# Summing the routed results of a two-layer mixture-of-experts kernel: TensorE takes six token tiles in pairs, VectorE ten, and ScalarE scales every anchor's result

## The chip, the cores and the metric

The kernel runs on one core of a Trainium2 chip. The metric is the device time of one execution in microseconds. In three runs the kernel before took 939.09, 937.78 and 936.85 us, a median of 937.78 us.

## The reference, cut to what matters

The network has two layers on 2048 tokens of width 256. Each layer is a cross attention followed by a mixture of experts, each added to its input. The change lies in the second layer's mixture of experts:

```python
x = x + L0_xattn(layernorm(x), ctx) ; x = x + L0_moe(layernorm(x))
x = x + L1_xattn(layernorm(x), ctx) ; x = x + L1_moe(layernorm(x))
...
# L1_moe, for 32 routed experts (6 per token) and 16 anchors (1 per token)
eo = (silu(x @ w_gate[e]) * (x @ w_up[e])) @ w_down[e]
routed = sum over the token's 6 experts of weight * eo
anchor = (silu(x @ a_gate[l]) * (x @ a_up[l])) @ a_down[l], l from the token's first expert
out = routed + shared + 0.1 * anchor
```

All of it is in float32.

## The kernel before, in words

The last stage handles the tokens of the second layer in gathered tiles of 128 rows: `T1` = 127 routed tiles, then `TA` = 31 anchor tiles, `NTL` = 158 in all (`ORDER` keeps their order). All engines run a loop over i, and each does the step of another tile in it.

- **SyncE** loads the gathered rows of tile i into the ring `RX` of eight buffers (L1054), 16 of the anchor tiles ahead into `RA`.
- **TensorE**, iteration i: it transposes tile i's rows (L859 to L863, two transposes at L332 and L333), multiplies gate and up of tile i-2 (`mm`, L328) and down of tile i-4 (L882). The transposed rows go to one of the three PSUM banks 0, 1 and 6 (`turned1`), so that transposing tile i waits for VectorE's copy of tile i-3. Gate and up are in banks 2, 3 and 7, down in banks 4 and 5.
- **VectorE**, iteration i: it scales the result of tile i-5 if that is an odd tile (`scale_odd`, L2107), copies tile i's transposed rows out (L2121), finds weights and destinations once per four tiles (`find`, L2083 to L2099), and multiplies silu(gate) by up for tile i-3 (L2131, anchors L2133).
- **ScalarE**, iteration i: it scales the result of tile i-5 if that is an even tile (`scale_even`, L1460), copies tile i+1's expert weights to a fixed place (`weights_copy`, L1451), and takes silu of tile i-2 (L1476, anchors L1478).
- **GpSimd** scatters each scaled result with an indirect DMA (L1134) to the tensor `yb1`, where each token has six places, or for an anchor to `yba`, where it has one. A scaled result stands in one of `NYT` = 6 buffers (`YTS`). `result(i)` gives the buffer and how many times its semaphore has counted; before a buffer is written again, the scatter that read it must have landed. `all_back` waits for the landing of the last six scatters, one per buffer.

When the results of all routed tiles are in `yb1`, SyncE loads them back (`yf_load(n)`, L1069) into `YF`, two token tiles of 128 at a time with 1536 values per row, in the order n = 2, 3, 6, 0, 1, 7, 4, 5. The last five of these loads stand in the queue among the last row loads of the ring, and so wait for them: n = 0, 1, 7 each come behind two of them, 4 and 5 behind 7. When the anchors' results have all landed too, it loads those (`YA`, L1090), four token tiles per load, groups 1, 0, 3, 2.

The sixteen token tiles of the output are then summed on two engines. VectorE takes the eleven of `DONE`: for each one add of 768 columns and three of 256 (`yf_add`, L2056 to L2068). It is a generator, of which one step (of five per tile) is taken in each iteration from i = 139, and what is left runs after the loop. Three adds of `YA` (L2144) then finish groups 1, 0 and 2. TensorE takes the five of `SUMMED` after its loop: for each it multiplies the identity by `X` (L890), by the six parts of `YF` (L894) and by `YA` (L897), into one PSUM bank, and ScalarE copies the bank to `X` (L1481). ScalarE sends groups 3 and 2 of the output (L1484), SyncE groups 1 and 0 (L1093).

Of the kernel before, what the change touches and what calls it, by code (L numbers as in the profile page):

```python
# [13 lines left out]
D = 256  # L14
# [5 lines left out]
E0 = 64  # L20
# [9 lines left out]
NEW = 22  # L30
EARLY, BESIDE = 1, 3
FRONT, HELD = 4, 18
NBX = 7
NB1 = 8
BATCH = 4
NYT = 6
BIG = 65536.0
SEG = 17
DUM = R1 * SEG
# [5 lines left out]
EPS = 1e-5  # L45
NTL = T1 + TA
NU = 2 * NT
AHEAD = 16
FIRST_P = T1 + 1
RINGED = list(range(FIRST_P)) + list(range(FIRST_P + AHEAD, NTL))  # L50
DONE = (4, 5, 6, 7, 0, 1, 2, 3, 8, 9, 10)
LEAD = 7
NR = 33856
SUMMED = (12, 13, 14, 15, 11)


def constants():
# [56 lines left out]
class Chain:  # L114
# [12 lines left out]
    ["l_c", "l_ct", "l_mask", "l_wr0", "l_s0", "l_sd", "l_small", "out"]  # L127
    + [f"l_x{i}" for i in range(4)] + ["l_" + n for n in WNAMES]
    + [f"sc{i}" for i in range(6)] + ["z_b0", "z_y0", "z_dum"]
    + [f"ew{i}" for i in range(NEW // 2)] + [f"bx{i}" for i in range(NBX)] + [f"yt{i}" for i in range(NYT)]  # L130
    + [f"yl{i}" for i in range(3)] + [f"w1_{i}" for i in range(8)] + ["wa"]
    + ["pad_s", "pad_t", "pad_a", "pad_b", "pad_c"] + [f"ya{i}" for i in range(4)]

# [14 lines left out]
def build(nc, a, out):  # L148
# [10 lines left out]
    with ExitStack() as ctx:  # L159
# [3 lines left out]
        PS = ctx.enter_context(nc.psum_tensor("PS", [P, 8, 512], F32))  # L163
# [6 lines left out]
        ident, upper, ones = cst("ident"), cst("upper"), cst("ones")  # L170
        X = sb("X", [P, NT, D])
        H2T = sb("H2T", [P, 2, NT * P])
        WS1 = sb("WS1", [P, 768])
# [4 lines left out]
        YT = sb("YT", [P, 3, D])  # L178
# [7 lines left out]
        AS_ = sb("AS_", [P, 4, 512])  # L186
# [34 lines left out]
        at = [0]  # L221
# [43 lines left out]
        ring_at = [for_l0 + 2048 + 768 * i if i < 17 else past + 768 * (i - 13) + 3072 * (i >= HELD) for i in range(NEW)]  # L265
        EWR = [R[:, o:o + 768] for o in ring_at]
        BXS = [BX[:, i, :] for i in range(4)] + [R[:, NR - ROW * i:NR - ROW * i + ROW] for i in (3, 2, 1)]
        YTS = [YT[:, i, :] for i in range(3)] + [AS_[:, 3, 0:D], AS_[:, 3, D:2 * D], AS_[:, 2, D:2 * D]]
        YTS0 = YTS[0:3] + [R[:, NR - 3 * ROW - D * i:NR - 3 * ROW - D * (i - 1)] for i in (3, 2, 1)]
        SG0L = R[:, late:late + 2048].rearrange("p (c n) -> p c n", c=2)  # L270
        SD0L = R[:, late + 2048:late + 3072].rearrange("p (c n) -> p c n", c=4)
# [72 lines left out]
        def result(i):  # L344

            j = i - E0
            s = i % NYT if j < 0 else j % NYT
            return s, i // NYT + 1 if j < 0 else (E0 - s + NYT - 1) // NYT + j // NYT + 1

        def all_back(w, i):  # L350

            for k in range(i - NYT + 1, i + 1):
                s, n = result(k)
                w.wait_ge(f"yt{s}", 16 * n)

        def routed(i):
            return ORDER[i] < T1
# [19 lines left out]

        def turned1(j):

            return PS[:, (0, 1, 6)[j % 3], 0:256]  # L380

        def hidden1(j):
            return PS[:, (2, 3, 7)[j % 3], :]

        def scaled1(j):

            return ("d_yt", j // 2 + 1) if j % 2 else ("a_yt", E0 + j // 2 + 1)

        def weight1(j):
            return MS[:, j // BATCH % 2, j % BATCH, 1:2]  # L390
# [60 lines left out]
        def _(e):  # L451
# [405 lines left out]
            for i in range(NTL + 4):  # L857
                if i < NTL:
                    regs[i] = e.value_load(TI[0:1, ORDER[i]:ORDER[i] + 1], min_val=0, max_val=(R1 if routed(i) else NA) - 1)  # L859
                    w.wait_ge(*landed(i))  # L860
                    if i > 2:
                        w.wait_ge("d_xt", E0 + i - 2)
                    tr2(e, turned1(i), rows_in(i, 1)[:, 0, 0:D]).then_inc(S["s_ta"], 1)  # L863
                if 0 <= i - 2 < NTL:
                    j, wd = i - 2, width(i - 2)
                    w.wait_ge("d_xt", E0 + j + 1)
                    w.wait_ge("a_gu", j + 1)
                    if j > 2:
                        w.wait_ge("d_ac", E0 + j - 2)
                    for o in range(2 if routed(j) else 1):  # L870
                        x = mm(e, hidden1(j)[:, o * P:o * P + P],
                               [(WG[j % 4][:, 2 * wd * k + o * P:2 * wd * k + o * P + P], XT1[:, j % 4, k, :]) for k in range(2)])
                    x.then_inc(S["s_g"], 1)
                if 0 <= i - 4 < NTL:
                    j = i - 4
                    w.wait_ge("d_ac", E0 + j + 1)
                    if j > 1:
                        w.wait_ge(*scaled1(j - 2))
                    if not routed(j):
                        w.wait_ge("p_at", 1)  # L880
                    left, src = (AC, W1[:, bass.ds(regs[j], 1), 512:768]) if routed(j) else (ACA, WD[:, bass.ds(regs[j], 1), :])
                    e.matmul(PS[:, 4 + j % 2, 0:256], left[:, j % 3, :], src.rearrange("p a n -> p (a n)"),  # L882
                             start=True, stop=True).then_inc(S["s_y"], 1)

            w.wait_ge("d_xt", E0 + NTL)
            w.wait_ge("d_ac", E0 + NTL)
            w.wait_ge(*scaled1(NTL - 2))
            w.wait_ge(*scaled1(NTL - 1))
            for at, n in enumerate(SUMMED):
                e.matmul(PS[:, at, 0:256], ident, X[:, n, :], start=True, stop=False)  # L890
            for at, n in enumerate(SUMMED):
                w.wait_ge(f"w1_{n // 2}", 32)
                for k in range(6):
                    e.matmul(PS[:, at, 0:256], ident, YF[:, n, k * D:k * D + D], start=False, stop=False)  # L894
            for at, n in enumerate(SUMMED):
                w.wait_ge(f"ya{n // 4}", 16)
                e.matmul(PS[:, at, 0:256], ident, YA[:, n, :], start=False, stop=True).then_inc(S["s_fin"], 1)  # L897


        @block.sync  # L900
# [284 lines left out]
        def _(e):  # L1185
# [264 lines left out]
                    w.wait_ge("s_g", E0 + j - 3)  # L1450
                e.copy(WG[j % 4][:, 0:4 * width(j)], src.rearrange("p a n -> p (a n)")).then_inc(S["a_gu"], 1)  # L1451

            def scale_even(j):
                w.wait_ge("s_y", E0 + j + 1)
                w.wait_ge("d_m", j // BATCH + 1)
                slot, n = result(E0 + j)
                w.wait_ge(f"yt{slot}", 16 * (n - 1))
                if slot > 2:
                    w.wait_ge("s_dn", 32)
                e.activation(YTS[slot], PS[:, 4 + j % 2, 0:256], ACT.Copy, scale=weight1(j)).then_inc(S["a_yt"], 1)  # L1460

            weights_copy(0)
            for i in range(NTL + 5):
                if i in (22, 34):
                    wa_load((i - 22) // 12)
                if 0 <= i - 5 < NTL and i % 2:
                    scale_even(i - 5)
                if i + 1 < NTL:
                    weights_copy(i + 1)
                if 0 <= i - 2 < NTL:  # L1470
# [5 lines left out]
                        e.activation(SL[:, j % 4, :], hidden1(j)[:, 0:P], ACT.Silu).then_inc(S["a_sl"], 1)  # L1476
                    else:
                        e.activation(SL[64:P, j % 4, :], hidden1(j)[0:64, 0:P], ACT.Silu).then_inc(S["a_sl"], 1)  # L1478
            def summed(at):
                w.wait_ge("s_fin", at + 1)  # L1480
                e.copy(X[:, SUMMED[at], :], PS[:, at, 0:256]).then_inc(S["a_fin"], 1)  # L1481

            def send(g):
                e.dma_start(out_d[:, 4 * g:4 * g + 4, :], X[:, 4 * g:4 * g + 4, :]).then_inc(S["out"], 16)  # L1484

            for at in range(4):
                summed(at)
            w.wait_ge("a_fin", 4)
            send(3)
            summed(4)  # L1490
            w.wait_ge("a_fin", 5)
            w.wait_ge("d_out", 3)
            send(2)
            w.wait_ge("out", 64)
# [3 lines left out]
        def _(e):  # L1498
# [613 lines left out]
            for i in range(NTL + 5):  # L2112
                b, part = divmod(i, BATCH)
                n = min(BATCH, NTL - BATCH * b)
                if 0 <= i - 5 < NTL and i % 2 == 0:
                    scale_odd(i - 5)
                if i < NTL:
                    w.wait_ge("s_ta", E0 + i + 1)
# [19 lines left out]
            for _ in adding:  # L2138
                pass
            for k, g in enumerate((1, 0, 2)):  # L2140
                ns = slice(4 * g, min(4 * g + 4, 11))
                w.wait_ge(f"ya{g}", 16)
                w.wait_ge("d_xf", min(4 * k + 4, 11))
                e.tensor_tensor(X[:, ns, :], X[:, ns, :], YA[:, ns, :], ALU.add).then_inc(S["d_out"], 1)  # L2144

def by_partition(gate, up, down=None):
# [49 lines left out]
```

## Time and profile before

| | us |
|---|---|
| median of three runs | 937.78 |
| the profiled execution, its own time | 935.34 |
| its span | 933.7 |
| TensorE busy | 833.1 (89%) |
| VectorE busy | 624.7 (67%) |
| GpSimd busy | 540.3 (58%) |
| ScalarE busy | 506.9 (54%) |

The times are those of one profiled execution, in microseconds from the start of the span. PE is TensorE's multiplication and PEld its loading of weights, DVE is VectorE, ACT ScalarE, POOL GpSimd, SP SyncE; a q behind the name is the engine's queue of DMA issues. A float32 multiplication by TensorE appears as two records. A row of the windows gives the stretch, its length, the busy time of PE, PEld, DVE, ACT and POOL with their instructions, the granted TensorE clock, the DMA engines' busy share and GB/s. A row of the timeline begins with start and length and ends with the idle time before it, in brackets. A row of the groups gives the count, then the busy time, the mean in ns, the idle time before and what ended it. An L number is the line of the kernel, and a line can be that of a helper: L328 is `mm`, L332 and L333 are the transposes.

The routed tiles of the second layer run until about 861 us, the anchor tiles from there to 909.7 us, and the last sums to the end at 933.7 us.

### The profile page before, as it was taken

The numbers are of one execution on the slowest core, as the hardware profiler recorded it, in microseconds if no ns is written. First come the engines' busy times: TensorE is split into PE (matmuls) and PEld (weight loads), VectorE is DVE, ScalarE is ACT, GpSimd is POOL, SyncE is SP. The second block draws the span as 40 slices with busy tenths as digits, with TensorE's granted clock in tenths as the row PEclk, the third lists the DMA queues.
The fourth block names the chain that finished last, engine by engine and source line by source line (L and its number), as shares of the span: only waits on it lengthen the run. The fifth ranks groups of instructions, "written<-read, shape, count | busy, mean of one in ns | idle before, by whom it ended". The sixth has DMA issues, their size and how long they took to land. (4 is left out here: it accounts for less than half of the span.)

```text
span 933.7 us, 23111 instructions
## 1 busy us (share of the span) xinstructions
PE 833.1 (89%) x6790; PEld 663.7 (71%) x6790; DVE 624.7 (67%) x2666; ACT 506.9 (54%) x1528; POOL 540.3 (58%) x526
## 2 busy tenths in 40 slices
PE   5798888877899999988999999778799999999887
PEld 2566666654479878846777777555698899999756
DVE  3678888765245555446699999967465555666896
ACT  2687777754023333344676666530466666666540
POOL 1005666777537777768325556667465566666660
PEclk9899999989999999999999999989899999999999
DMA  9974522104799999765002242399778666664696
GB/s 315 345 247 160 183 81 73 44 22 170 248 284 314 322 318 202 114 178 181 24 30 91 88 145 110 141 422 329 217 243 298 209 193 195 191 194 113 245 382 222
DMA packets 112557, 183.98 MB, mean 197 GB/s; under 512 B 18456, under 2 KB 88170, under 8 KB 110899
## 3 DMA queue, kind: packets, MB, share of 16 engines
q1 hardware_dynamic: 79506, 125.32, 40.6%
q0 software_dynamic: 28704, 49.37, 18.5%
q10 hardware_dynamic: 4224, 7.82, 2.4%
q8 instruction: 57, 0.93, 0.4%
q14 instruction: 66, 0.53, 0.2%
HBM read 106.91 MB, written 90.86 MB: 212 GB/s over the span
## 5 line engine op out<-in xcount | busy, mean ns | idle before, releaser
L1122 POOL DMA_INDIRECT buf<-R,RI x240 | 236.4, 985 | 207.4 <-PE PS L564 137.6
L328 PE MATMUL PS<-R 128*128 128x256 f32 (+2 forms) x352 | 109.4, 440 | 14.1 <-DMA R<-in_ctxT 10.5
L1272 ACT ACTIVATE R<-R,MX 128x120 f32<-128x120 f32 x256 | 80.2, 387 | 32.3 <-DVE MX L1595 32.3
L2121 DVE COPY H2T<-PS 128x256 f32<-128x256 f32 x158 | 66.3, 419 | 44.1 <-PE PS L333 43.4
L328 PEld LDWEIGHTS PS<-R 128*128 128x128 f32 (+1 forms) x352 | 64.0, 200 | 43.9 <-issue 34.4
L1272 ACT ACTIVATE R<-PS,MX 128x120 f32<-128x120 f32 x256 | 71.5, 367 | 43.4 <-DVE MX L1595 43.4
L1134 POOL DMA_INDIRECT yb<-YT,DI x64 | 62.4, 975 | 38.8 <-issue 29.5
L1134 POOL DMA_INDIRECT yb<-AS_,DI x63 | 61.3, 973 | 37.6 <-issue 34.1
L328 PE MATMUL PS<-H2T,SS_ 128*128 128x128 f32 x576 | 79.3, 279 | 0.0
L882 PE MATMUL PS<-R,AC 128*128 x254 | 76.1, 381 | 0.7 <-issue 0.4
L328 PE MATMUL PS<-H2T,AS_ 128*128 128x128 f32 x564 | 75.7, 275 | 0.0
L328 PEld LDWEIGHTS PS<-H2T,SS_ 128*128 128x128 f32 x576 | 72.8, 196 | 0.1
L526 PE MATMUL PS<-R 64*128 64x240 f32 x512 | 69.7, 391 | 3.2 <-ACT R L1272 1.4
L1146 POOL DMA_INDIRECT yb<-YT,DI x33 | 50.9, 1543 | 34.0 <-DVE DI L1782 24.9
L328 PEld LDWEIGHTS PS<-H2T,AS_ 128*128 128x128 f32 x564 | 69.1, 192 | 0.0
L542 PE MATMUL PS<-C,R 128*120 128x128 f32 x512 | 67.9, 276 | 0.0
L328 PEld LDWEIGHTS PS<-XT,R 128*128 128x128 f32 x512 | 63.8, 192 | 5.7 <-issue 5.3
L328 PE MATMUL PS<-XT,R 128*128 128x128 f32 x512 | 67.6, 275 | 0.0
L1476 ACT ACTIVATE SL<-PS 128x128 f32<-128x128 f32 x127 | 35.2, 277 | 56.5 <-PE PS L328 50.8
L564 PE MATMUL PS<-R 120*32 120x128 f32 x1024 | 42.6, 285 | 25.5 <-ACT R L1283 16.3
L1283 ACT COPY R<-PS 120x512 f32<-120x512 f32 x96 | 54.6, 577 | 17.1 <-PE PS L542 17.0
L542 PEld LDWEIGHTS PS<-C,R 128*120 128x120 f32 x512 | 59.6, 140 | 5.7 <-issue 1.6
(234 smaller groups left out, 1973.9 us busy)
## 6 DMA issues: line engine op xcount, KB each, us to landing
R<-in_ew SPq DMA_DIRECT2D x64, 384.0 KB, 5.8
H2T<-buf SPq DMA_DIRECT2D x142, 140.0 KB
R<-in_w SPq DMA_DIRECT2D x8, 1536.0 KB, 15.9
R<-yb SPq DMA_DIRECT2D x8, 1536.0 KB, 12.0
buf<-Z SPq DMA_DIRECT2D x8, 1120.0 KB, 13.6
yb<-Z SPq DMA_DIRECT2D x17, 512.0 KB, 3.3
R<-yb SPq DMA_DIRECT2D x16, 512.0 KB, 3.4
R<-buf SPq DMA_DIRECT2D x43, 140.0 KB, 2.5
```

What stands on the lines that cost most here:

```text
L328: m = e.matmul(out_, left, right, start=(i == 0), stop=(i == len(pairs) - 1))
L526: x = e.matmul(ps_scores(l, u, half)[:, 2 * c:2 * c + 2, :], QT[r, s, c, (n % 2) * P:(n % 2) * P + P], KALL[r, u % 2, c, b, :, :], start=T ...
L542: x = e.transpose(PS[0:SK, 3 + half, i * P:i * P + P], SM[:, z, 4 * half + i, :], ident)
L564: x = e.matmul(PS[32 * q:32 * q + 32, 6, 256 * what + P * c:256 * what + P * c + P], left, PT[0:SK, 2 * (u % 2) + half, 2 * c + side, :], ...
L882: e.matmul(PS[:, 4 + j % 2, 0:256], left[:, j % 3, :], src.rearrange("p a n -> p (a n)"), start=True, stop=True).then_inc(S["s_y"], 1)
L1122: e.indirect_dma_start(out=(buf1 if l else buf0)[:, :], out_offset=bass.IndirectOffsetOnAxis(ap=RI[:, n % 6, k:k + 1].bitcast(U32), axis=0 ...
L1134: e.indirect_dma_start(out=yb[:, :], out_offset=bass.IndirectOffsetOnAxis(ap=DI[:, i - E0:i - E0 + 1].bitcast(U32), axis=0), in_=YTS[resul ...
L1146: e.indirect_dma_start(out=yb0[:, :], out_offset=bass.IndirectOffsetOnAxis(ap=DI[:, i:i + 1].bitcast(U32), axis=0), in_=YTS0[result(i)[0]] ...
L1272: x = e.activation(SM[:, z, h, :], src[:, i, :], ACT.Exp, bias=MX[:, z, h:h + 1])
L1283: e.copy(PT[0:SK, r, :, :], PS[0:SK, 3 + half, :].rearrange("p (h t) -> p h t", h=4)).then_inc(S["a_pt"], 1)
L1476: e.activation(SL[:, j % 4, :], hidden1(j)[:, 0:P], ACT.Silu).then_inc(S["a_sl"], 1)
L2121: e.tensor_copy(XT1[:, i % 4, :, :], two(turned1(i))).then_inc(S["d_xt"], 1)
```

## The change

TensorE's part of the sums goes from five token tiles to six, taken in pairs of neighbours, so that each multiplication by the identity has 512 columns in place of 256. The first pair (12, 13) is summed in bank 6, which `turned1` gives up (it keeps banks 0 and 1, so that transposing tile i waits for the copy of tile i-2), by seven multiplications in the iterations 149, 151, ... 161. The pairs (14, 15) and (10, 11) come behind the loop, and the three multiplications of `YA` last. VectorE keeps ten token tiles. Second-layer results have eight buffers in place of six. ScalarE scales all anchors' results and the even routed ones, VectorE the odd routed ones alone.

```diff
+NY1 = 8
+AMONG = NTL - 9
-DONE = (4, 5, 6, 7, 0, 1, 2, 3, 8, 9, 10)
+DONE = (4, 5, 6, 7, 0, 1, 2, 3, 8, 9)
-SUMMED = (12, 13, 14, 15, 11)
+SUMMED = (12, 14, 10)
...
-        YTS = [YT[:, i, :] for i in range(3)] + [AS_[:, 3, 0:D], AS_[:, 3, D:2 * D], AS_[:, 2, D:2 * D]]
+        YTS = [YT[:, i, :] for i in range(3)] + [AS_[:, 3, 0:D], AS_[:, 3, D:2 * D], AS_[:, 2, D:2 * D], WS1[:, 0:D], WS1[:, D:2 * D]]
...
         def result(i):
             j = i - E0
-            s = i % NYT if j < 0 else j % NYT
-            return s, i // NYT + 1 if j < 0 else (E0 - s + NYT - 1) // NYT + j // NYT + 1
+            if j < 0:
+                return i % NYT, i // NYT + 1
+            s = j % NY1
+            return s, j // NY1 + 1 + (len(range(s, E0, NYT)) if s < NYT else 0)
...
-            for k in range(i - NYT + 1, i + 1):
+            for k in range(i - (NYT if i < E0 else NY1) + 1, i + 1):
...
         def turned1(j):
-            return PS[:, (0, 1, 6)[j % 3], 0:256]
+            return PS[:, j % 2, 0:256]
+        def total1(pair):
+            return PS[:, (6, 0, 1)[pair], :].rearrange("p (t n) -> p t n", t=2)
+        def results1(pair, k):
+            n = SUMMED[pair]
+            return X[:, n:n + 2, :] if k == 0 else YF[:, n:n + 2, (k - 1) * D:k * D] if k < 7 else YA[:, n:n + 2, :]
...
+        def on_act(j):
+            return not routed(j) or j % 2 == 0
         def scaled1(j):
-            return ("d_yt", j // 2 + 1) if j % 2 else ("a_yt", E0 + j // 2 + 1)
+            n = sum(on_act(k) for k in range(j + 1))
+            return ("a_yt", E0 + n) if on_act(j) else ("d_yt", j + 1 - n)
...
-                    if i > 2:
-                        w.wait_ge("d_xt", E0 + i - 2)
+                    if i > 1:
+                        w.wait_ge("d_xt", E0 + i - 1)
...
+                k, odd = divmod(i - AMONG, 2)
+                if 0 <= k < 7 and odd == 0:
+                    if k:
+                        w.wait_ge(f"w1_{SUMMED[0] // 2}", 32)
+                    e.matmul(total1(0), ident, results1(0, k), start=(k == 0), stop=False)
             w.wait_ge("d_xt", E0 + NTL)
             w.wait_ge("d_ac", E0 + NTL)
             w.wait_ge(*scaled1(NTL - 2))
             w.wait_ge(*scaled1(NTL - 1))
-            for at, n in enumerate(SUMMED):
-                e.matmul(PS[:, at, 0:256], ident, X[:, n, :], start=True, stop=False)
...
-                for k in range(6):
-                    e.matmul(PS[:, at, 0:256], ident, YF[:, n, k * D:k * D + D], start=False, stop=False)
...
-                e.matmul(PS[:, at, 0:256], ident, YA[:, n, :], start=False, stop=True).then_inc(S["s_fin"], 1)
+            for pair in (1, 2):
+                for k in range(7):
+                    if k:
+                        w.wait_ge(f"w1_{SUMMED[pair] // 2}", 32)
+                    e.matmul(total1(pair), ident, results1(pair, k), start=(k == 0), stop=False)
+            for pair in range(3):
+                w.wait_ge(f"ya{SUMMED[pair] // 4}", 16)
+                e.matmul(total1(pair), ident, results1(pair, 7), start=False, stop=True).then_inc(S["s_fin"], 1)
...
-                if 0 <= i - 5 < NTL and i % 2:
-                    scale_even(i - 5)
+                if 0 <= i - 5 < NTL and on_act(i - 5):
+                    scale_here(i - 5)
...
-                e.copy(X[:, SUMMED[at], :], PS[:, at, 0:256]).then_inc(S["a_fin"], 1)
+                e.copy(X[:, n:n + 2, :], total1(pair)).then_inc(S["a_fin"], 1)
...
-                if 0 <= i - 5 < NTL and i % 2 == 0:
+                if 0 <= i - 5 < NTL and not on_act(i - 5):
                     scale_odd(i - 5)
...
-                ns = slice(4 * g, min(4 * g + 4, 11))
+                ns = slice(4 * g, min(4 * g + 4, 10))
```

## Rows read from the trace of the kernel before

**Rows 1.** Windows of a routed stretch, the last anchors and their end: busy per engine
```profile
800.00:820.00 20.00, 20.00 (x157) 18.70 (x156) 11.96 (x47) 13.74 (x33) 12.59 (x14) 1.00 0.64 187
...
889.60:904.00 14.40, 12.63 (x77) 9.30 (x76) 13.59 (x41) 7.59 (x22) 8.92 (x10) 1.00 1.01 403
904.00:909.70 5.70, 3.21 (x14) 1.79 (x14) 5.06 (x15) 1.49 (x4) 4.13 (x4) 0.97 1.02 409
```

**Rows 2.** Timeline, routed tiles: transposes of a tile, its copy, transposes two tiles on
```profile
800.80 0.27 PE L332 MATMUL PS<-C,H2T 128*128 128x128 f32 x1
801.40 0.41 DVE L2121 COPY H2T<-PS 128x256 f32<-128x256 f32 x1
803.89 0.27 PE L332 MATMUL PS<-C,H2T 128*128 128x128 f32 x1
```

**Rows 3.** Timeline, transposes of two neighbouring anchors, then of tiles 149 and 157
```profile
862.18 0.27 PE L332 MATMUL PS<-C,R 128*128 128x128 f32 x1
863.28 0.27 PE L332 MATMUL PS<-C,R 128*128 128x128 f32 x1
...
889.61 0.32 PE L332 MATMUL PS<-C,H2T 128*128 128x128 f32 x1
902.45 0.32 PE L332 MATMUL PS<-C,H2T 128*128 128x128 f32 x1 [0.22 <-issue]
```

**Rows 4.** Timeline, GpSimd: first and last scatter of the 31 anchors
```profile
866.37 0.98 POOL L1134 DMA_INDIRECT yba<-YT,DI  x1 [0.30 <-ACT YT L1460]
911.93 0.97 POOL L1134 DMA_INDIRECT yba<-YT,DI  x1 [0.30 <-issue]
```

**Rows 5.** Groups of instructions by shape, 864 to 909.5 us: mean ns, idle before
```profile
L2107 DVE TENSOR_SCALAR AS_<-PS,H2T 128x256 f32<-128x256 f32 x10 | 4.8, 484 | 0.3
L1460 ACT ACTIVATE YT<-PS,H2T 128x256 f32<-128x256 f32 x11 | 5.2, 474 | 4.0 <-PE PS L882 2.3 <-DMA yba<-YT,DI 1.7
L1451 ACT COPY AS_<-R 128x256 f32 x12 | 4.8, 400 | 3.6 <-issue 3.6
L1478 ACT ACTIVATE SL<-PS 64x128 f32<-64x128 f32 x29 | 7.8, 269 | 9.2 <-PE PS L328 8.7
```

**Rows 6.** Timeline, VectorE's wait for the first results, and TensorE after it
```profile
875.51 0.96 DVE L2056 TENSOR_TENSOR R<-R 128x768 f32<-128x768 f32 x1 [1.47 <-DMA R<-yb]
...
877.90 0.69 PE L882 MATMUL PS<-R,H2T 128*128 x2 [2.02 <-DVE H2T L2133]
```

**Rows 7.** Lines L1069 and L1090: loads of `YF` and `YA`, issue and landing
```profile
L1069 SPq DMA_DIRECT2D R<-yb x8: 382/464/563, 869.1 to 893.8; - x8
DMA to landing us min/median/max: 6.4/12.0/20.6
...
L1090 SPq DMA_DIRECT2D R<-yba x4: 359/500/507, 914.9 to 916.4; - x4
DMA to landing us min/median/max: 4.0/5.6/7.0
```

**Rows 8.** The chain that ended last, its last parts: start, length, what
```profile
902.67 6.32 DMA yba<-YT,DI
...
909.72 3.89 PE PS L890 x10
913.61 12.95 PE PS L894 x60
926.56 1.74 PE PS L897 x8
```

**Rows 9.** Timeline, VectorE's last adds and ScalarE's last issue
```profile
922.58 3.22 DVE L2144 TENSOR_TENSOR X<-X,R 128x1024 f32<-128x1024 f32 x3
...
929.59 0.40 ACTq L1484 DMA_DIRECT2D out<-X  x1
```

**Rows 10.** Groups by shape, 400 us to the end: instructions of 512 columns
```profile
L328 PE MATMUL PS<-H2T,WS 128*128 128x512 f32 x32 | 15.0, 607 | 0.0
L1408 ACT ACTIVATE SS_<-PS 128x512 f32<-128x512 f32 x4 | 2.4, 597 | 17.9 <-PE PS L328 17.9
```

More of the change, by code:

```diff
@@ L129 @@
     + [f"sc{i}" for i in range(6)] + ["z_b0", "z_y0", "z_dum"]
-    + [f"ew{i}" for i in range(NEW // 2)] + [f"bx{i}" for i in range(NBX)] + [f"yt{i}" for i in range(NYT)]
+    + [f"ew{i}" for i in range(NEW // 2)] + [f"bx{i}" for i in range(NBX)] + [f"yt{i}" for i in range(NY1)]
     + [f"yl{i}" for i in range(3)] + [f"w1_{i}" for i in range(8)] + ["wa"]
@@ L888, in _ @@
             w.wait_ge(*scaled1(NTL - 1))
-            for at, n in enumerate(SUMMED):
-                e.matmul(PS[:, at, 0:256], ident, X[:, n, :], start=True, stop=False)
-            for at, n in enumerate(SUMMED):
-                w.wait_ge(f"w1_{n // 2}", 32)
-                for k in range(6):
-                    e.matmul(PS[:, at, 0:256], ident, YF[:, n, k * D:k * D + D], start=False, stop=False)
-            for at, n in enumerate(SUMMED):
-                w.wait_ge(f"ya{n // 4}", 16)
-                e.matmul(PS[:, at, 0:256], ident, YA[:, n, :], start=False, stop=True).then_inc(S["s_fin"], 1)
+            for pair in (1, 2):
[6 more added lines that the diff above has]
+                e.matmul(total1(pair), ident, results1(pair, 7), start=False, stop=True).then_inc(S["s_fin"], 1)
         @block.sync
@@ L1451, in weights_copy, with scale_here @@
                 e.copy(WG[j % 4][:, 0:4 * width(j)], src.rearrange("p a n -> p (a n)")).then_inc(S["a_gu"], 1)
-            def scale_even(j):
+            def scale_here(j):
                 w.wait_ge("s_y", E0 + j + 1)
@@ L1478, in _, with summed @@
                         e.activation(SL[64:P, j % 4, :], hidden1(j)[0:64, 0:P], ACT.Silu).then_inc(S["a_sl"], 1)
-            def summed(at):
-                w.wait_ge("s_fin", at + 1)
-                e.copy(X[:, SUMMED[at], :], PS[:, at, 0:256]).then_inc(S["a_fin"], 1)
+            def summed(pair):
+                n = SUMMED[pair]
+                w.wait_ge("s_fin", pair + 1)
+                e.copy(X[:, n:n + 2, :], total1(pair)).then_inc(S["a_fin"], 1)
             def send(g):
                 e.dma_start(out_d[:, 4 * g:4 * g + 4, :], X[:, 4 * g:4 * g + 4, :]).then_inc(S["out"], 16)
-            for at in range(4):
-                summed(at)
-            w.wait_ge("a_fin", 4)
+            for pair in range(2):
+                summed(pair)
+            w.wait_ge("a_fin", 2)
             send(3)
-            summed(4)
-            w.wait_ge("a_fin", 5)
+            summed(2)
+            w.wait_ge("a_fin", 3)
             w.wait_ge("d_out", 3)
@@ L2140, in _ @@
             for k, g in enumerate((1, 0, 2)):
-                ns = slice(4 * g, min(4 * g + 4, 11))
+                ns = slice(4 * g, min(4 * g + 4, 10))
                 w.wait_ge(f"ya{g}", 16)
-                w.wait_ge("d_xf", min(4 * k + 4, 11))
+                w.wait_ge("d_xf", min(4 * k + 4, 10))
                 e.tensor_tensor(X[:, ns, :], X[:, ns, :], YA[:, ns, :], ALU.add).then_inc(S["d_out"], 1)
```

## The prediction, made before the changed kernel ran

> **What bounds the kernel now.** I read the windows first. In the routed tiles TensorE is busy 20.00 of 20 us while VectorE has 11.96 and ScalarE 13.74 [rows 1]: TensorE sets the pace there, 1.55 us a tile (transposes at 800.80, and two tiles on at 803.89) [rows 2]. In the anchors it is different. TensorE alone could do one in 1.10 us (862.18 to 863.28), but from tile 149 to tile 157 eight tiles took 12.84 us, 1.61 each [rows 3]. In that stretch VectorE is busy 13.59 of 14.40 us, and ScalarE 7.59 [rows 1]. So VectorE, which has begun its share of the sums there, sets the pace.
>
> GpSimd is next. A scatter takes 0.98 us and the one behind it starts 0.30 us later, so 31 need at least 31 x 1.28 = 39.7 us; from 866.37 to 912.90 they took 46.5 [rows 4]. 6.8 us of that are waits for scaled results.
>
> Then the end, from the chain: after a scatter's landing (6.32 us) TensorE starts the sums at 909.72 and ends them near 928.7, in 10, 60 and 10 records [rows 8]. A sum of 256 columns takes 12.95/30 = 0.43 us, but the first five take 3.89 us, 0.78 each. Ahead of them TensorE was busy only 3.21 of 5.70 us [rows 1]. Two other chains end a little earlier: `YA` is issued from 914.92 on and the last load lands 7.0 us after its issue at 916.4, at 923.4 [rows 7]; VectorE's last adds run from 922.58 to 925.80 [rows 9].
>
> **The change, part by part.**
>
> **Fewer columns behind the loop.** TensorE's 40 sums of 256 columns cost 40 x 0.43 = 17.3 us and 1.7 for the slow start, 19.0 in all [rows 8]. The 24 of 512 have no row of their own. A record of 512 columns lasts 592 to 607 ns, mostly as depth of the pipeline [rows 10]; the bounds are 0.60 us (two records wholly overlapped) and 1.21 us (not at all) for each sum. I take 0.86, twice the 0.43, because that row is the same operation. Seven among the anchors are 6.0 us; 17 behind are 14.6. That alone is 4.4 us off TensorE's end.
>
> **Seven sums among the anchors.** Five fall in iterations 149 to 157, 5 x 0.86 = 4.3 us, so TensorE wants 1.10 + 0.48 = 1.58 us a tile there, as much as the 1.61 that it takes now. They cost nothing against today's pace, but cap the gain in these iterations: if VectorE's cover of 0.5 us a tile goes, they cost up to 4.3 us. The other two fall where TensorE is idle 2.5 of 5.7 us [rows 1]. Their operands (tiles 12, 13) are the third load issued at about 870, long landed by 890.
>
> **No scaling on VectorE.** 16 scalings of 0.484 us go [rows 5], 0.24 us a tile: VectorE's need falls from some 1.5 (13.59/9 tiles) to 1.27 us. ScalarE gets 15 more, and needs 0.47 + 0.40 + 0.27 = 1.14 us a tile, plus about 0.17 in waits for the multiplication: 1.31. GpSimd needs 1.28. Three engines near 1.3 that wait on one another will not run at 1.3; I take 1.4 for iterations 142 to 148 and 1.55 for 149 to 157. Before 142 nothing moves: VectorE waits for the first `YF` load until 875.51, and TensorE resumes at 877.90 after 2.02 us idle [rows 6]. I save 0.4 us there (the scaling ahead of the copy), 1.3 up to 149, 0.5 up to 157: transposes of 157 at 900.3 in place of 902.45.
>
> **The drain.** From there to the sums it took 7.3 us, with both last scalings waiting for a buffer. VectorE no longer scales between its adds, and the buffers are there; four iterations of 1.3 remain, 5.3 us. The sums behind the loop start at 905.6, 4.1 earlier.
>
> **Eight buffers.** A scatter that lands 6.32 us after its issue [rows 8] is later than five more take (5 x 1.28 = 6.4), so six buffers just stall; eight give 10.2 us. This is what lets GpSimd come near its 1.28. I take its last scatter's issue at 906.7, against 911.93. In the routed tiles, where a scatter starts only every 1.55 us, it changes nothing.
>
> **Two banks for the transposes.** TensorE now waits for the copy of tile i-2 ahead of the transposes in place of just behind them. In the routed tiles that copy ends at 801.81 and the transposes that would wait start at 803.89 [rows 2]: 2.08 us to spare, cost 0. If the copy were ever that late, it would cost at most the transposes themselves (two of 0.27 us, which then can't run during the wait) in each tile. I take 0.
>
> **VectorE's sums.** One token tile less is 0.96 + 3 x 0.42, 2.1 us from start to start; with the earlier start VectorE finishes its ten near 917 and is no bound.
>
> **What is late next.** First, the `YF` load of tiles 10 and 11 is issued last, at 893.8, and lands 20.6 us later, at 914.4 [rows 7]. The DMA engines are at 1.01 of their share there [rows 1], so it moves only with its issue, 1.2 us, to 913.2. Tile 11 stood last in TensorE's order; now pair (10, 11) does. TensorE does pair (14, 15) from 905.6 to 911.6, waits to 913.2, and ends six more at 918.4. Second, `YA`. The last scatter goes out at 906.7, takes 0.97, and lands 5.3 us later in the full queue, at 913.0; 8.5 us from first issue to last landing [rows 7] gives 921.5. So `YA` takes over as the bound: 0.86 for the last sum, 0.6 for ScalarE's copy of 512 columns [rows 10], and 4.2 from its last issue to the end (929.59 to 933.7) [rows 9]: 927.2, **6.5 us less**.
>
> The rule on the clock in the Trainium skill ("TensorE: Matmul & The Clock Gate", Part 1) is that the array is throttled by default and only sustained work releases it. By that rule the two sums in the drain would keep the full clock, as the slow first five seem to show (0.78 us each against 0.43); the wait for `YA` could bring the half clock back for the last three sums, some 2.6 us more than my sum by the same two rows.
>
> **The sum.** 933.7 - 6.5 = 927.2 of span. The profiled execution took 935.34, 2.4 below the median of 937.78, so I set the gain against the median: **931.3 us**.
>
> **Rivals.**
>
> *The anchors don't get shorter.* For it: three engines within 0.05 us of one another and sums that bring TensorE to 1.58; and a scatter that lands only when the last `YF` load has drained (914.4) would hold `YA` whatever GpSimd does. Against: VectorE's 0.24 us is plain. Then `YA` lands at 923.4 as now, the end is 923.4 + 0.9 + 0.6 + 4.2 = 929.1, 4.6 less: 933.2 us. The half clock in the last sums gives much the same from the forecast's own case.
>
> *GpSimd runs at its floor.* Last scatter at 905.3, `YA` at 920, 8 us less: 929.8. It is inside the forecast's own range, 928.5 to 932.5.
>
> *ScalarE becomes the bound, and the kernel slower.* Every scaling now stands in its order between silu and the weights' copy, and waits for its multiplication. The idle ahead of its scalings was 4.0 us over 11, and ahead of the weights' copies 3.6 over 12 [rows 5]. With 0.4 of the one and 0.15 of the other in each tile it needs 1.14 + 0.55 = 1.7 us, and the sums in TensorE's order hold the multiplication by another 0.43 in nine of them. That is 31 x 0.17 (1.7 against 47.5/31 = 1.53) + 3.9 = 9.2 us, less 4.6: 942.4 us. It makes the kernel slower from 1.74 us a tile. Against it: ScalarE is idle half of the time there [rows 1], and part of its idle time is VectorE's lateness.
>
> *The change is there but nothing shows.* For instance ScalarE at 1.65, which gives back the 4.6: 937.5 us.
>
> **How the numbers follow.** Forecast 0.58 (with the floor case in it), anchors no shorter 0.25, nothing shows 0.08, slower 0.09. The measurement can tell about 0.2%, 1.9 us. The first two cases are faster, and a little of the third: faster 0.84, same 0.08, slower 0.08. The range takes in the forecast and the first rival with half a microsecond or so of spread beyond each, and the bounds of the 512-column sum where TensorE would bind (17 x 0.35 us more lands at 933 to 935): 928.0 to 935.0.
>
> **What would show it.** In the trace after: transposes of 149 and 157 12.4 us apart or less; no VectorE scaling behind tile 126; GpSimd's last scatter near 907; TensorE's sums behind the loop in records 0.43 us apart, with an idle gap ahead of the last three, ended by a landing of `YA`; the routed pace unchanged at 1.55. Wrong if ScalarE is busy over 90% in the anchors, if the last `YA` lands later than 923, or if the routed pace moves: 127 tiles make 1.3 us of each hundredth.

## The result: 0.5% faster, with the last sums now waiting for the anchors' results

The changed kernel took 931.46 us (median of eight runs, 930.55 to 935.18). The kernel before, run beside it, took 936.86 us (eight runs, 933.99 to 939.09). The ratio is 0.995, 95% interval 0.9932 to 0.9967: 4.7 us faster, between 3.1 and 6.4 (the two medians lie 5.4 us apart). The forecast was 931.3 us in a range of 928.0 to 935.0, so the time is met. But the forecast was a gain of 6.5 us from a median of 937.78, and the kernel before came out 0.9 us lower in the larger sample; the gain is smaller than forecast by 1 to 2 us.

The profiled execution has a span of 930.6 us against 933.7, and that difference alone misleads. The expert stage of the second layer began later in it: the first transposes start at 660.45 us against 657.55, in code that the change doesn't touch. The routed tiles take 200 to 204 us from one execution to another. The yardstick for the rest of this text is therefore the start of tile 128's transposes, near the beginning of the anchors (127 is the first of their tiles; 862.06 us after, 859.54 before), from which single executions differ by about 1 us where nothing should (two_banks, below).

| us from tile 128's transposes to | before | forecast | after |
|---|---|---|---|
| transposes of tile 157 | 42.9 | 40.8 | 41.4 |
| first sum behind the loop | 50.2 | 46.1 | 47.8 |
| issue of the last scatter, its end | 53.4 | 48.1 | 51.2 |
| first issue of the `YA` loads | 55.4 | 53.5 | 53.9 |
| end of the span | 74.2 | 67.7 | 68.5 |

The windows of the changed kernel, answering to [rows 1] (same columns), show the routed pace kept, VectorE relieved in the late anchors, and TensorE without a gap in the drain, the iterations behind tile 157's transposes:

```profile
800.00:820.00 20.00, 20.00 (x157) 18.70 (x156) 12.16 (x46) 13.21 (x32) 12.64 (x13) 1.00 0.66 188
...
889.60:904.00 14.40, 13.86 (x82) 10.29 (x81) 11.68 (x34) 9.51 (x28) 10.24 (x11) 1.00 1.02 388
904.00:909.80 5.80, 5.80 (x28) 3.99 (x27) 5.49 (x16) 3.29 (x9) 3.85 (x4) 1.00 1.02 416
```

VectorE is busy 11.68 us where it was 13.59, ScalarE 9.51 where it was 7.59. TensorE, 12.63 before, has 13.86 with its new sums. In the drain it is busy 5.80 of 5.80 us at full clock, where it was idle for 2.5, and the sums behind the loop start without a slow half. Whether that is owed to the two sums in the drain is another matter: anchors_only (below) has none there, and its sums behind the loop start at full clock too. The windows of the first sums behind the loop, of the kernel before and then of anchors_only:

```profile
909.70:913.60 3.90, 3.88 (x11) 3.23 (x12) 3.80 (x8) 0.00 (x0) 2.71 (x2) 0.61 0.83 319
906.90:909.20 2.30, 2.25 (x11) 2.02 (x12) 2.23 (x5) 0.00 (x0) 1.69 (x3) 1.00 1.03 408
```

The timeline at the end, TensorE, ScalarE and the queues (the brackets hold the idle time ahead and what ended it), answering to [rows 8, 9]:

```profile
909.81 1.06 PE L917 MATMUL PS<-X,C 128*128 128x512 f32 x2
910.71 5.31 PE L917 MATMUL PS<-R,C 128*128 128x512 f32 x12
...
915.98 2.01 SPq L1113 DMA_DIRECT2D R<-yba  x4
916.72 5.31 PE L917 MATMUL PS<-R,C 128*128 128x512 f32 x12
921.22 1.88 SPq L1116 DMA_DIRECT2D out<-X  x2
922.99 2.84 PE L920 MATMUL PS<-R,C 128*128 128x512 f32 x6 [0.96 <-DMA R<-yba]
...
926.70 0.40 ACTq L1508 DMA_DIRECT2D out<-X  x1
```

Before, TensorE went from sum to sum to its end. Now it is through with the routed results at 922.0, waits 0.96 us, and its last three sums follow landings of `YA`. Twelve records of 512 columns take 5.15 us from 910.71 to 915.86, 0.86 us a sum, as taken.

What holds the issue of the `YA` loads? It waits for the landing of the last eight scatters. Line L1092 issues the `YF` loads; its issues and their landings, answering to [rows 7]:

```profile
L1092 SPq DMA_DIRECT2D R<-yb x8: 382/469/674, 870.4 to 895.0; - x8
DMA to landing us min/median/max: 7.4/12.4/20.5
```

The last `YF` load, issued at 895.0, lands 20.5 us later, near 915.5. The last scatter's issue ended at 913.27, it landed at 915.90, and the `YA` loads follow at 915.98. Before, the last `YF` load landed at 914.5 and the `YA` loads followed at 914.92. The experiments show this distance again and again (below): it is the last `YF` load, and not GpSimd's last scatter, that `YA` follows.

GpSimd's scatters, from the same timeline, with VectorE's adds that lie beside them:

```profile
885.05 0.96 DVE L2080 TENSOR_TENSOR R<-R 128x768 f32<-128x768 f32 x1
885.30 1.56 POOL L1157 DMA_INDIRECT yba<-AS_,DI  x1 [0.30 <-ACT AS_ L1483]
887.16 0.97 POOL L1157 DMA_INDIRECT yba<-AS_,DI  x1 [0.30 <-issue]
...
891.99 0.96 DVE L2080 TENSOR_TENSOR R<-R 128x768 f32<-128x768 f32 x1
892.52 1.27 POOL L1157 DMA_INDIRECT yba<-YT,DI  x1 [0.30 <-ACT YT L1483]
...
904.94 0.97 POOL L1157 DMA_INDIRECT yba<-YT,DI  x1 [1.41 <-ACT YT L1483]
...
911.91 1.36 POOL L1157 DMA_INDIRECT yba<-AS_,DI  x1 [0.30 <-issue]
```

The 31 scatters take 44.4 us in place of 46.5, where 39.7 is the floor. Most follow the one before by 0.30 us: up to tile 148 GpSimd, not VectorE, sets the pace but for a wait of VectorE for the first `YF` load. In the last anchors TensorE, busy 13.86 of 14.40 us with its five sums, is as near to being the bound. Several scatters are longer than 0.97 us, and one waits 1.41 us, behind TensorE's wait for a row load that came late (total, times, longest):

```profile
PEld PS L334 <- DMA H2T<-buf: 1.2, 1, 1.2
```

### The profile page after: what moved, and what is told of

Same layout as the page of the kernel before. It is cut to its first block and busy times, and to the rows that moved or that the text cites. A ratio compares the mean times of both kernels' runs of the same rounds, so it can differ in the third digit from the quotient of the medians.

```text
span 930.6 us, 23058 instructions
## 1 busy us (share of the span) xinstructions
PE 833.6 (90%) x6758; PEld 658.2 (71%) x6758; DVE 617.5 (66%) x2646; ACT 513.5 (55%) x1542; POOL 540.3 (58%) x526
## 5 line engine op out<-in xcount | busy, mean ns | idle before, releaser
L544 PE MATMUL PS<-R 64*128 64x240 f32 x512 | 69.5, 390 | 3.2 <-ACT R L1295 1.4
L1169 POOL DMA_INDIRECT yb<-YT,DI x33 | 50.9, 1542 | 35.9 <-DVE DI L1806 29.4
L330 PEld LDWEIGHTS PS<-H2T,AS_ 128*128 128x128 f32 x564 | 69.1, 192 | 0.0
L1306 ACT COPY R<-PS 120x512 f32<-120x512 f32 x96 | 54.6, 577 | 20.3 <-PE PS L560 20.1
L560 PEld LDWEIGHTS PS<-C,R 128*120 128x120 f32 x512 | 61.6, 143 | 5.9 <-issue 1.8
L1157 POOL DMA_INDIRECT yb<-YT,DI x48 | 46.7, 973 | 32.6 <-issue 23.3
L1157 POOL DMA_INDIRECT yb<-AS_,DI x48 | 46.6, 971 | 26.9 <-issue 25.9
## 6 DMA issues: line engine op xcount, KB each, us to landing
R<-yb SPq DMA_DIRECT2D x8, 1536.0 KB, 12.4
```

What stands on the lines that cost most here:

```text
L330: m = e.matmul(out_, left, right, start=(i == 0), stop=(i == len(pairs) - 1))
L544: x = e.matmul(ps_scores(l, u, half)[:, 2 * c:2 * c + 2, :], QT[r, s, c, (n % 2) * P:(n % 2) * P + P], KALL[r, u % 2, c, b, :, :], start=T ...
L560: x = e.transpose(PS[0:SK, 3 + half, i * P:i * P + P], SM[:, z, 4 * half + i, :], ident)
L1157: e.indirect_dma_start(out=yb[:, :], out_offset=bass.IndirectOffsetOnAxis(ap=DI[:, i - E0:i - E0 + 1].bitcast(U32), axis=0), in_=YTS[resul ...
L1169: e.indirect_dma_start(out=yb0[:, :], out_offset=bass.IndirectOffsetOnAxis(ap=DI[:, i:i + 1].bitcast(U32), axis=0), in_=YTS0[result(i)[0]] ...
L1306: e.copy(PT[0:SK, r, :, :], PS[0:SK, 3 + half, :].rearrange("p (h t) -> p h t", h=4)).then_inc(S["a_pt"], 1)
```

## The experiments

Theory at the outset: TensorE's sums set the end before; the change takes columns from behind the loop and lets the anchors' results come earlier; now their landing sets the end. The table gives, from tile 128's transposes in each profiled execution, the end of the last scatter's issue, the landing of the last `YF` load, the first issue of `YA` loads, and the end of the span. The diffs are against the changed kernel unless said otherwise, and `...` stands for lines left out.

| kernel | last scatter | last `YF` landing | `YA` issue | end | ratio to before (95%) |
|---|---|---|---|---|---|
| before | 53.4 | 54.9 | 55.4 | 74.2 | 1 |
| changed | 51.2 | 53.5 | 53.9 | 68.5 | 0.995 (0.9932 to 0.9967) |
| sums_only | 52.6 | 54.1 | 54.5 | 69.3 | 0.9962 (0.9947 to 0.9977) |
| anchors_only | 52.2 | 54.8 | 55.0 | 71.1 | 0.9979 (0.9958 to 1.0) |
| six_buffers | 50.2 | 52.4 | 52.8 | 67.4 | 0.9952 (0.9933 to 0.9971) |
| split_scaling | 52.5 | 54.2 | 54.6 | 69.5 | 0.9956 (0.994 to 0.9971) |
| two_banks | 52.2 | 53.9 | 54.3 | 73.0 | one execution |
| pair_behind | 51.4 | 53.2 | 53.7 | 73.4 | 0.9999 (0.9979 to 1.0018) |
| adds_behind | 50.9 | 52.9 | 53.4 | 73.8 | one execution |
| loads_late | 49.7 | 78.3 | 50.9 | 92.5 | one execution |
| ya_order | 51.6 | 53.7 | 54.1 | 70.5 | 0.9959 (0.9942 to 0.9976) |
| rows_first | 50.0 | 52.9 | 53.1 | 67.8 | 0.9954 (0.9931 to 0.9978) |
| both_orders | 49.8 | 52.9 | 53.2 | 69.1 | 0.9958 (0.994 to 0.9976) |

The intervals of the faster kernels overlap; between them only the traces tell, and those to about 1 us.

One reading runs through the whole table. In the twelve kernels that issue all `YF` loads first, `YA` is issued 0.2 to 0.5 us behind the last `YF` landing, while it is anywhere from 1.9 to 3.5 us behind the end of the last scatter's issue. In loads_late, where five `YF` loads are issued behind `YA`, it is 1.2 us behind the scatter's. With the `YF` loads ahead of it, the last scatter lands when they have drained, wherever between 49.8 and 53.4 us GpSimd is through with it. Why a small scatter is held by larger loads, no run here shows.

**sums_only**: the new sums, with neither the buffers nor ScalarE's share.

```diff
-NY1 = 8
+NY1 = 6
...
-            return not routed(j) or j % 2 == 0
+            return j % 2 == 0
```

> The changed kernel with six buffers and with odd anchors scaled by VectorE as before: the new sums alone. Yardstick within one trace: from the first transposes of the second layer's expert stage to the end of the span, 276.2 us before and 270.2 in the changed kernel. Theory (TensorE's sums behind the loop set the end before, and 4.4 us of columns go): the anchors take what they took, YA lands as before, and the stage takes 272.0 us, about 4 us less than before; ratio near 0.9955. Rival (the five sums among the anchors cost there what they save behind): 275 to 276 us, ratio 0.999 to 1.

Measured: ratio 0.9962, and 69.3 us from tile 128 against 74.2. (The whole stage took 273.4 us, with 2 us more than before in the routed tiles, which is why the later comparisons leave those out.) The sums alone bring some 4.8 of the 5.6 us, and the five among the anchors don't give it back: the theory holds.

**anchors_only**: the change without its sums.

```diff
-DONE = (4, 5, 6, 7, 0, 1, 2, 3, 8, 9)
-SUMMED = (12, 14, 10)
+DONE = (4, 5, 6, 7, 0, 1, 2, 3, 8, 9, 10)
+SUMMED = (12, 13, 14, 15, 11)
...
-            return PS[:, j % 2, 0:256]
+            return PS[:, (0, 1, 6)[j % 3], 0:256]
```

> The kernel before with eight buffers and ScalarE scaling all anchors, its sums and its three transpose banks kept. Theory (TensorE starts its sums 2 to 4 us earlier and still sets the end): 272.5 to 274 us of stage, ratio near 0.997. Rival (GpSimd's chain was the bound in the anchors all along, or ScalarE takes VectorE's place): 276 us, ratio 1.

Measured: 271.7 us of stage (1.4 of the 4.4 us less than before lie in the routed tiles) and 71.1 from tile 128, 3.1 less than before; ratio 0.9979, whose interval reaches 1. The sums start 1.6 us earlier, and these, with the slow start gone (granted clock 1.00, above), still set the end. The two parts are not additive (4.8 and 3.1 against 5.6 together): each moves TensorE's end, each removes the slow start, which can be saved but once, and beyond a point `YA` holds the end.

**six_buffers**: buffers undone, all else kept.

```diff
-NY1 = 8
+NY1 = 6
...
```

> The changed kernel with six buffers in place of eight, all else kept. Theory (a scatter that lands over 6 us after its issue stalls the sixth one after): GpSimd's last scatter 1 to 2 us later, stage 271 to 272.5 us against 270.2. Rival (GpSimd issues at its floor either way, buffers add only slack): 270.2 us, same as the changed kernel.

Measured: last scatter at 50.2 us, a stage of 268.2 us, and the end at 67.4 from tile 128, no later than with eight; ratio 0.9952 against 0.995. The rival holds: the two more buffers bring nothing that can be seen. The waits of this kernel from 855 us on (total, times, longest) show how little they save:

```profile
ACT AS_ L1483 <- DMA yba<-AS_,DI: 1.1, 2, 0.9
```

ScalarE does wait for a landing, twice and for 1.1 us in all, and GpSimd's last scatter is no later for it.

**split_scaling**: VectorE scales odd anchors again.

```diff
-            return not routed(j) or j % 2 == 0
+            return j % 2 == 0
```

> The changed kernel with odd anchors scaled by VectorE again, eight buffers kept. Theory (VectorE set the pace of the later anchors): pace back from about 1.53 to 1.6 us a tile, last scatter 2 us later, stage 272 us. Rival (with TensorE's five sums at 1.5 us a tile and GpSimd at 1.3 to 1.4, VectorE's scaling is covered): 270.2 us.

Measured: the last scatter ends 1.3 us later than in the changed kernel and the end comes 1.0 later. With six buffers the same step (sums_only against six_buffers) is 2.4 and 1.9 us. Both go the theory's way, at half to all of its size, but a step of 1 us is no more than single traces differ by; the ratios (0.9956 and 0.995) can't tell them apart.

**two_banks**: the kernel before with two transpose banks.

```diff
-            return PS[:, (0, 1, 6)[j % 3], 0:256]
+            return PS[:, j % 2, 0:256]
...
-                    if i > 2:
-                        w.wait_ge("d_xt", E0 + i - 2)
+                    if i > 1:
+                        w.wait_ge("d_xt", E0 + i - 1)
```

> The kernel before with two transpose banks in place of three, nothing else. Theory (the copy is 2 us early in every routed tile): steady routed pace 1.546 us a tile as before, from the transposes of tile 128 to the end 74 us as before (74.2). Rival (TensorE's transposes are held by the copy): a pace of 1.6 or more, or 0.3 us a tile more in the anchors, 80 us or more.

This diff is against the kernel before. Its transposes, two tiles apart:

```profile
800.05 0.27 PE L332 MATMUL PS<-C,H2T 128*128 128x128 f32 x1
...
803.14 0.27 PE L332 MATMUL PS<-C,H2T 128*128 128x128 f32 x1
```

3.09 us for two tiles, as in [rows 2], and 73.0 us to the end against 74.2: no cost. The 1.2 us between them are also a measure of how far single traces of one kernel can be trusted.

**pair_behind**: the first pair's seven sums behind the loop too.

```diff
-                if 0 <= k < 7 and odd == 0:
+                if False:
...
-            for pair in (1, 2):
+            for pair in (0, 1, 2):
```

> The changed kernel with the first pair's seven sums moved behind the loop: all 24 come after the last anchor. From tile 128 to the end 68.5 us in the changed kernel. Theory (TensorE's sums then end 6 us later, of which 1 us was waiting for the anchors' results; the anchors themselves run at most 1 us faster without them): 73 us, ratio near 1. Rival (the sums among the anchors cost what they save): 68.5 to 70 us.

TensorE's sums behind the loop in this kernel's timeline, the three pairs and the last three:

```profile
910.23 5.31 PE L917 MATMUL PS<-R,C 128*128 128x512 f32 x12
915.38 1.02 PE L917 MATMUL PS<-X,C 128*128 128x512 f32 x2
916.24 5.31 PE L917 MATMUL PS<-R,C 128*128 128x512 f32 x12
921.39 1.02 PE L917 MATMUL PS<-X,C 128*128 128x512 f32 x2
922.25 5.31 PE L917 MATMUL PS<-R,C 128*128 128x512 f32 x12
927.40 2.74 PE L920 MATMUL PS<-R,C 128*128 128x512 f32 x6
```

73.4 us, ratio 0.9999: the gain is gone. TensorE is the bound again, without a wait ahead of the last three. Pairs of 512 columns and a sixth token tile bring nothing by themselves (anchors_only, without them, ends 2.3 us earlier); that seven sums lie where TensorE had room is worth 4.9 us. Up to tile 157 the anchors took 41.4 us with them and 41.6 without, but that does not show the five to be free there: without them two waits for row loads, of 1.7 us (VectorE) and 1.6 us (TensorE), fill the room, and no run here has neither the sums nor these waits. (Sums of 256 columns among the anchors were not tried.)

**adds_behind** and **loads_late** ask what keeps GpSimd from its floor.

```diff
-                if i >= ROUTED + 12:
+                if False:
                     next(adding)
```

> The changed kernel with VectorE's adds all behind its loop. Asks what holds GpSimd in the anchors, which needs 44.4 us for 31 scatters where its floor is 39.7. Theory A (VectorE's adds: they delay the products that TensorE waits for, and with them the scaled results): the last scatter's issue ends 47 to 48 us after the transposes of tile 128, against 51.2, and scatters of 1.1 to 1.6 us are gone if the adds lengthen them. Theory B (the DMA queues, full of the results' loads, hold GpSimd and the row loads): 50.5 to 51 us, and the long scatters stay. The end comes later in both, since ten token tiles (21 us) then begin behind the loop.

```diff
-            for n, after in ((0, 2), (1, 2), (7, 2), (4, 0), (5, 0)):
-                for i in range(after):
-                    bx1_load(RINGED[FIRST_P + NB1 + (0, 2, 4)[(0, 1, 7).index(n)] + i])
-                yf_load(n)
+            for i in range(6):
+                bx1_load(RINGED[FIRST_P + NB1 + i])
...
+            for n in (0, 1, 7, 4, 5):
+                yf_load(n)
...
-                if i >= ROUTED + 12:
+                if ROUTED + 12 <= i < ROUTED + 31:
```

> The changed kernel with the last five loads of routed results issued behind the anchors' results, and VectorE taking only 19 of its steps in the loop. Theory A (VectorE's adds hold the anchors): last scatter's issue ends 50.5 to 51.2 us after tile 128's transposes, little changed. Theory B (the loads fill the DMA queues): no scatter over 1.0 us once the first three loads have landed, no wait for a row load, the last at 48 to 49 us, and the last scatter's landing 2 us after its issue's end. The end comes some 15 us later in both, with 7.5 MB still to load.

Without the adds, GpSimd runs at its floor for 22 anchors in a row, each 0.97 or 0.98 us and 0.30 behind the last, while the results' loads go on as before. Then it stops: first a row of the waits of adds_behind (total, times, longest), then two of its timeline,

```profile
DVE H2T L2107 <- DMA H2T<-buf: 2.8, 1, 2.8
```

```profile
894.94 0.97 POOL L1157 DMA_INDIRECT yba<-AS_,DI  x1 [0.30 <-issue]
898.22 0.97 POOL L1157 DMA_INDIRECT yba<-AS_,DI  x1 [2.30 <-ACT AS_ L1483]
```

VectorE waits 2.8 us for a row load, one of those issued behind a result load, and GpSimd, 2.3 us idle, ends at 50.9: what the adds no longer cost, the late rows do. With the loads late instead, no wait for a row load is left and GpSimd ends at 49.7, but long scatters remain, with the DMA engines busy 0.43 of the time in 880 to 905 us. One of them from the timeline of loads_late, with its add:

```profile
882.46 0.96 DVE L2080 TENSOR_TENSOR R<-R 128x768 f32<-128x768 f32 x1
882.92 1.34 POOL L1157 DMA_INDIRECT yba<-AS_,DI  x1 [0.30 <-ACT AS_ L1483]
```

So neither theory alone. With no late row load GpSimd's last scatter comes 1.2 to 1.5 us earlier (rows_first below, and loads_late). The lengthened scatters add 2.4 us in the changed kernel (32.5 us for 31, against 30.1 at 0.97 each), but adds_behind gains only 0.3, since its wait for a row is longer; both together were not taken away. What loads_late does settle is the landing: without the `YF` loads ahead of it the last scatter has landed, and `YA` goes out, 1.2 us behind the end of the issue, where 2 us were expected:

```profile
908.75 0.98 POOL L1157 DMA_INDIRECT yba<-AS_,DI  x1 [0.31 <-issue]
...
910.91 2.04 SPq L1111 DMA_DIRECT2D R<-yba  x4
```

**ya_order**, **rows_first** and **both_orders** try to go on from there.

```diff
-            for g in (1, 0, 3, 2):
+            for g in (3, 2, 1, 0):
...
-            for k, g in enumerate((1, 0, 2)):
+            for k, g in enumerate((2, 1, 0)):
...
```

> The changed kernel with the anchors' results loaded in the order of groups 3, 2, 1, 0 in place of 1, 0, 3, 2, and VectorE's last adds in the order 2, 1, 0. Theory (the last landing of these loads sets the end, and TensorE's three last sums, two copies behind one another and the sends hang on it): TensorE's last sums start without a wait, near 922.0 - 862.1 = 59.9 us after tile 128's transposes, and the end comes at 67.8 us against 68.5. Rival (the output's own writes fill the DMA queues, whichever goes first): 68.5 us.

```diff
-            for n, after in ((0, 2), (1, 2), (7, 2), (4, 0), (5, 0)):
+            for n, after in ((0, 2), (1, 4), (7, 0), (4, 0), (5, 0)):
...
```

> The changed kernel with the last two row loads put ahead of the second of the five late result loads. Theory (the row load of tile 156 lands 9 us late because it stands behind 3 MB of results, and GpSimd then idles 1.4 us): no wait for a row load at tile 156, last scatter's issue ends at 50 us after tile 128's transposes against 51.2, and the end at 67.5 to 68 us. Rival (the results' loads then end some 2 us later, and the last pair's sums wait for them): 68.5 to 70 us.

In ya_order TensorE's last sums do start without a wait, and ScalarE's last send is issued at 923.07 us, but 6.7 us ahead of the end, where in the changed kernel it is 3.9. Nothing is won: 70.5 us. The windows of its last stretch:

```profile
919.00:923.00 4.00, 3.20 (x8) 1.14 (x6) 2.96 (x3) 1.71 (x3) 0.00 (x0) 1.00 0.70 218
923.00:927.00 4.00, 0.00 (x0) 0.00 (x0) 0.15 (x1) 0.04 (x1) 0.00 (x0) 0.84 1.03 340
927.00:929.80 2.80, 0.00 (x0) 0.00 (x0) 0.00 (x0) 0.00 (x0) 0.00 (x0) 0.50 0.70 231
```

All four parts of the output are now sent within 1.5 us and move at 340 GB/s while the engines have next to no work; in the changed kernel two of them went out while the anchors' results still came in. The transfers fill the end, as the rival says, but their order is not without effect: neither 67.8 nor the rival's 68.5 us came. From the first `YA` issue to the end it is 14.6 us in the changed kernel and in rows_first, and 16.4 in ya_order.

In rows_first the wait at tile 156 is gone and the last scatter ends at 50.0 us, as the theory has it; the end, 67.8 us, is within its 67.5 to 68. But `YA` goes out only 0.8 us earlier, as the last `YF` load lands 0.6 us earlier, and not the 1.2 us of the last scatter. The ratio, 0.9954, is not better than the changed kernel's.

The edit of both_orders is the two above and `NY1 = 6`.

> Both reorderings with six buffers. If each gives what its theory says: 66.5 to 67 us from tile 128's transposes to the end, ratio to the kernel before near 0.993. If neither does: 67.4 to 68.5 us, ratio 0.995.

Measured 69.1 us and 0.9958. The two don't add up: the last scatter and `YA`'s issue come as in rows_first, and from there to the end it takes 15.9 us, near ya_order's 16.4 and not 14.6.

**rows_first_six** is rows_first with `NY1 = 6`.

> The changed kernel with the last row loads ahead of the second late result load and with six buffers, its order of the anchors' loads kept. Theory (the end follows the issue of the anchors' result loads by a fixed 14.6 us, as it did in the changed kernel and in the one with the row loads first; the issue follows the last scatter; eight buffers add nothing): from tile 128's transposes 53 us to that issue, 67.6 us to the end, ratio 0.994 to 0.995. Rival (eight buffers matter once the row loads are out of the way): issue at 54 to 55 us, the end at 69 us, ratio 0.997.

When it ran, both kernels took over 11% longer than in all other runs (1045.86 us for the kernel before, 1042.11 for it), for a reason that no run shows. The ratio is 0.9975 (0.9945 to 1.0005), and the anchors take at least 8 us longer than elsewhere (63.2 us to the `YA` issue), so it says nothing on buffers. The 14.8 us from there to the end agree with the fixed 14.6. That the issue follows the last scatter, as this expectation has it, is not what the table shows. No version measured here beats the changed kernel beyond its interval.

## Why the prediction was right, and where it was not

- **What bounded the kernel before**: right for the end, which TensorE's sums set; pair_behind puts the sums back behind the loop and with them the whole time. That VectorE set the pace of the late anchors is shown in direction only: in three pairs of kernels (before and anchors_only, which has the buffers too; split_scaling and changed; sums_only and six_buffers) the last scatter is 1.1, 1.3 and 2.4 us earlier where VectorE is spared the scaling.
- **Sums of 512 columns at 0.86 us, 17 of them behind the loop**: right, 0.86 us. (A record of 512 columns was read as "mostly" depth of the pipeline; at 0.43 us from start to start, most of its 607 ns was not.) The slow start went too: TensorE's granted clock is 1.00 in both windows above. The two sums in the drain are not shown to be the reason, since anchors_only and pair_behind, without them, have 1.00 there as well. The half clock that the rule of the Trainium skill ("TensorE: Matmul & The Clock Gate", Part 1) could have brought back in the wait for `YA` did not come; that wait was 0.96 us, and the granted clock of the last sums 1.00. Its price was mis-summed too: three sums at 2 x 0.78 in place of 0.86 us make 2.1 us and not 2.6.
- **Five sums among the anchors cap the gain at 1.58 us a tile**: right in size. From 149 to 157 the transposes took 12.9 us, where 12.4 was forecast, 1.61 a tile as before. The forecast of 1.55 was below its own cap, but between these transposes lie only four of the five sums; rows_first and loads_late, without the late row load, took 12.5 and 12.4 us.
- **VectorE's scaling**: right in direction, 1 to 2 us at the end where it was given 2.2 (1.3 + 0.5 + 0.4) in the anchors and more in the drain. (ScalarE gets 16 more scalings, not 15.)
- **Eight buffers as "what lets GpSimd come near its 1.28"**: wrong. six_buffers is as fast. The 6.32 us landing in the chain was real, but it is shorter than the 6.4 us of five more scatters, where the prediction calls it later; the waits for landings in six_buffers are 1.1 us and leave GpSimd's last scatter where it was.
- **The last scatter's issue at 906.7, 5.2 us earlier than 911.93**: this step was off the most. It came 49.8 us after tile 128's transposes in place of 52.4, 2.5 earlier. Two costs were missing in the sum: scatters that lengthen under VectorE's adds (32.5 us for 31, against 31.4 before and 30.1 at 0.97 each) and a row load that came late for tile 156.
- **The landing 5.3 us after the issue's end, and `YA` behind it**: it was 2.6, and `YA`'s issue, forecast at 53.5 us, came at 53.9. That looks like two errors that cancel, but they have one cause. `YA` follows the last `YF` landing, and that was forecast well, at 53.7 us (913.2), and came at 53.5. The prediction had this in a rival, "a scatter that lands only when the last `YF` load has drained", and its sum reached nearly the same time on another path. So the early scatter had little part in the gain: `YA` moved by 1.5 us, as the last `YF` landing did (54.9 to 53.5).
- **`YA` takes over as the bound**: right, landing to landing, and the end 0.8 us behind the forecast's 67.7.
- **ScalarE as the bound**: not seen; it is busy 9.51 of 14.40 us. (The rival's figures don't agree with one another: with its 3.9 us for the sums, 1.65 us a tile would have given back 7.6 us and not 4.6.) The rival that the anchors don't get shorter is half true: 1.5 us less to tile 157, 2.4 to the first sum, and `YA` is held by the `YF` loads as it says.

Measured against the larger sample, the forecast's gain of 6.5 us lies just above the interval (3.1 to 6.4). That 931.46 came so near to 931.3 is in part luck: the path to `YA` by the last scatter was wrong and gave the right time, and the reference was 0.9 us too high.

## What to carry to other kernels

Before pairing or widening the last work of an engine, ask whether it can move to where that engine idles: here the place of seven sums was worth 4.9 of 5.6 us, and wide sums left behind the loop none. Find out behind which wait the next chain stands before adding buffers or speeding up its producer: here small scatters landed with the large loads issued some 20 us ahead of them, and an earlier scatter brought little. Where loads and stores fill the end, an order that makes the last computation ready earlier may only bunch the stores.

## What the runs showed of the hardware

An indirect DMA that GpSimd begins while VectorE adds two operands out of SBUF lasts longer by about the rest of that add, less some 0.12 us. In the changed kernel one begun at 885.30, with an add running to 886.01 (0.71 us more), takes 1.56 us in place of 0.97; one begun at 892.52, with 0.43 us of an add left, takes 1.27. In the kernel before, the scatter at 909.89 meets an add that began at 909.83 and takes 1.74. One that begins just ahead of an add (911.93 and 911.95 in the kernel before), or beside none, keeps 0.97, and with the adds behind the loop 27 anchors' scatters in a row did. In the kernel before only two of the 31 anchors' scatters took over 1.1 us, in the changed kernel eight; why so few met an add before was not tried.

The Trainium skill ("SBUF — State Buffer", "Who interferes with whom") says that a VectorE instruction with two SBUF inputs contends with a GpSimd instruction that reads SBUF, and it calls the shared pair of ports an exclusive lock; it also reports a test in which such an add did not stall a DMA. The first agrees with these traces: the issue waits for the rest of the add to about 0.1 us. For an indirect DMA the second does not: here the add does hold it.
